# SiLU kept in its PSUM bank, GpSimd making the rests, and 23 divided down products in place of 15: an attention and mixture-of-experts kernel

## The chip, the cores and the metric

One core of a Trainium2 chip runs the whole program. The metric is the device time of one execution in microseconds. The engines are TensorE (PE in the profile; its weight loads are PEld), VectorE (DVE), ScalarE (ACT), GpSimd (POOL) and SyncE (SP), which issues most transfers. They run their own streams in order and wait for each other by semaphores.

## The reference

Inputs are x of 8 batches x 256 tokens x 128 features and a context of 8 x 256 x 96. All is float32. What is computed, cut to what matters:

```
x = x + attention(layernorm(x), ctx)       # scores normalised by their mean and variance over a batch, then softmax
h = layernorm(x)
out = x + swiglu(h @ sw1 + sb1) @ sw2 + sb2                       # the shared expert
        + sum over 8 experts e: cw[e] * (swiglu(h @ rw1[e] + rb1[e]) @ rw2[e] + rb2[e])
swiglu(a, b) = silu(a) * b;  cw: softmax of the router's logits, kept for the best two experts, else 0
```

All eight experts are computed for all tokens and weighted with cw, most of which is 0.

## The kernel before

The 2048 tokens go in four chunks c of 512 (two batches). For each chunk the nine experts e (e = 0 is the shared one) follow one another, which gives 36 slots n = 9c + e. The attention, second normalisation and router of the next chunks are laid between the slots, by the tables PE_AT, ACT_AT, DVE_AT and POOL_AT: a piece, the slot at which it stands and a place in it. Each engine's order is thus fixed in the source, and what an engine issues waits for what is queued ahead of it.

One slot n does this:

- TensorE: hidden(n, 0) and hidden(n, 1), the two halves of the hidden layer, of 128 x 512 into a PSUM bank each. To keep precision at the faster format fp32r, a factor is split into a head (rounded to fp32r) and a rest (what the rounding left), and three products are summed: head x head, rest x head, head x rest.
- ScalarE: expert_silu, the SiLU of the first half, into an SBUF buffer silu (L588).
- VectorE: expert_gate. First the weighting, silu times cw_all (L873), then the gate, (second half + bias) x silu, into act (L881). For e = 0 there is no weighting. For e = 1 in chunks 1 to 3, first_expert_gate makes the gate first (L858) and the weighting after it (L862).
- TensorE, three slots later (two near the end): down(n), which adds act times w2 to the bank OUT_B. A direct down is one float32 product (two rows in the trace). A divided one is three fp32r products and needs act_head, cast by ScalarE (L580), and act_rest, subtracted by VectorE (L890), besides w2_head and w2_rest (L886).

DIVIDED lists the divided downs: 8, 9, 10, 11, 16, 17, 18, 25, 26 and 27 to 32. The other 21 are direct. Down 33 stands in slot 35 between hidden(35, 0) and hidden(35, 1); the downs of slots 34 and 35 go straight to token order at the end (L998, w_sb<-act with 128 x 128).

Around this stand the steps that the prediction names: x_copy and the other copies of the next chunk's inputs, scores_average (the mean of the scores, bank<-sim_mom), scores_moments (sim_sq, sim_ex, sim_mom: small operations on VectorE, L743 to L750), normalise (xn, L541, which needs ln_shift, L722, and ln_rstd of GpSimd, L419), transpose_x2, x2_heads (ScalarE, L547) and x2_rests (VectorE, L799), router (bank<-gate_parts), router_logits to router_weights on VectorE, which ends in cw_cols (L850), and transpose_cw (L1113), whose result is written to memory and read back as cw_all, spread over all partitions. GpSimd makes powers (row_powers L410, ln_rstd L419, sim_r L425) and the rests of w1 (L434); in most slots it has nothing to do.

transpose_cw(c) stands at the end of slot 9c - 1, so chunk 1's in slot 8, chunk 2's in slot 17, chunk 3's in slot 26. The semaphores that matter: a_ps and b_ps count hidden halves, silu_sb SiLUs, scaled_sb weightings, act_sb gates, act_head_sb and act_rest_sb the parts of act, y_ps downs.

## Time and profile before

| | |
|---|---|
| median of 3 runs | 135.35 us (135.25 to 135.39) |
| the profiled execution | 135.15 us, of it span 133.4 us |
| TensorE's granted clock | 1.00 of full speed |
| busy: PE, DVE, ACT, POOL | 127.5, 107.6, 84.8, 23.9 us |
| SiLU (L588), 35 of 128 x 512 | 0.69 us each |
| weighting (L873), 26 of 128 x 512 | 0.69 us each |
| gate (L881), 32 of 128 x 512 | 0.75 us each |
| act_head (L580), act_rest (L890), 15 each | 0.62 and 0.68 us each |

A line of a timeline is one instruction or a run of equal ones: start, duration, engine, source line, operation, what it writes and reads, and in brackets the idle time of the engine before it with what ended it. TensorE's matmuls overlap in the record: one lasts 0.40 us but the next starts 0.23 us later, so starts are what to compare.

### The profile page before, as it was taken

The page shows a single profiled execution, that of the slowest core. Times are in us where ns is not written, and L with a number is a line of the kernel's source. Part 1 is how long each engine was busy: PE and PEld are TensorE (multiplying, and loading weights), DVE is VectorE, ACT ScalarE, POOL GpSimd, SP SyncE. Part 2 cuts the span into 40 slices and gives each one's busy share as a digit, 9 for nine tenths or more (in the row PEclk, how much of TensorE's full clock was granted, in tenths as well). Part 3 has the DMA queues.
Part 4 walks back from the last instruction along what each step waited for, and adds up shares of the span by engine and source line. Part 5 has one row for each costly group of instructions (what it writes and reads, how often), then busy time and mean ns, then how long its engine had stood idle before and what let it go on. Part 6 is the DMA issues. An engine that isn't in the chain of part 4 may idle for free.

```text
span 133.4 us, 2135 instructions
## 1 busy us (share of the span) xinstructions
PE 127.5 (96%) x632; PEld 96.7 (72%) x632; DVE 107.6 (81%) x313; ACT 84.8 (64%) x165; POOL 23.9 (18%) x41
## 2 busy tenths in 40 slices
PE   7899999889999999999999999999999999999992
PEld 7677796858577776686788676598677667788871
DVE  1497788696997989999759997699697879989872
ACT  1557978996265389947653299956633987647250
POOL 7184154057700020602100020001200000000000
PEclk9999999999999999999999999999999999999999
DMA  3999400002910000098000002087000207910022
GB/s 107 304 331 269 149 7 0 0 2 86 337 59 0 0 0 2 10 296 328 0 5 0 0 0 79 18 292 332 2 0 0 79 5 182 403 44 5 0 79 79
DMA packets 8828, 12.97 MB, mean 97 GB/s; under 512 B 1321, under 2 KB 6994, under 8 KB 8306
## 3 DMA queue, kind: packets, MB, share of 16 engines
q1 hardware_dynamic: 8242, 12.62, 28.1%
q10 hardware_dynamic: 576, 0.23, 0.6%
q8 instruction: 5, 0.08, 0.3%
q14 instruction: 5, 0.04, 0.1%
HBM read 11.73 MB, written 1.11 MB: 96 GB/s over the span
## 4 chain that ended last, share of the span: by engine, by line
PE 61%; issue 15%; DVE 9%; ACT 7%; POOL 6%; DVEq 0%; POOLq 0%; ACTq 0%
PE bank L998 55%; ACT prob L508 3%; POOL w_rest L434 3%; POOL ln_rstd L419 2%; PE bank L1062 1%; PE bank L1014 1%; ACT L553 1%; PE bank L1113 1%; PE bank L1090 1%; DVE x L902 1%; ACT act_head L580 1%; PE bank L1181 1%; DVE g_beats L824 1%; DVE g_rank L827 1%; ACT silu L588 1%
## 5 line engine op out<-in xcount | busy, mean ns | idle before, releaser
L588 ACT ACTIVATE silu<-bank,b_cols 128x512 f32<-128x512 f32 (+1 forms) x37 | 24.8, 676 | 23.7 <-PE bank L998 23.2
L998 PE MATMUL bank<-x_head,w_head 128*128 128x512 f32 x72 | 33.7, 468 | 0.3 <-issue 0.3
L998 PE MATMUL bank<-x_head,w_rest 128*128 128x512 f32 x72 | 28.5, 395 | 0.0
L998 PE MATMUL bank<-x_rest,w_head 128*128 128x512 f32 x72 | 28.5, 395 | 0.0
L881 DVE SCALAR_TENSOR_TENSOR act<-bank,b_cols,silu 128x512 f32<-128x512 f32 (+1 forms) x34 | 24.9, 734 | 1.3 <-DVE silu L873 0.3
L873 DVE TENSOR_TENSOR silu<-silu,cw_all 128x512 f32<-128x512 f32 (+1 forms) x28 | 18.6, 668 | 3.3 <-ACT silu L588 2.6
L998 PE MATMUL bank<-act,w_sb 128*128 128x512 f32 x38 | 19.4, 592 | 0.0
L998 PEld LDWEIGHTS bank<-x_head,w_head 128*128 128x128 f32 x72 | 13.6, 189 | 5.3 <-issue 2.7
L998 PEld LDWEIGHTS bank<-x_rest,w_head 128*128 128x128 f32 x72 | 13.6, 189 | 3.9 <-issue 1.9
L998 PEld LDWEIGHTS bank<-x_head,w_rest 128*128 128x128 f32 x72 | 13.5, 188 | 3.3
L890 DVE TENSOR_TENSOR act_rest<-act,act_head 128x512 fp32r<-128x512 f32 x15 | 10.0, 685 | 4.1 <-ACT silu L588 2.0
L580 ACT CAST act_head<-act 128x512 fp32r<-128x512 f32 x15 | 9.0, 623 | 1.2 <-DVE act L862 0.6
L419 POOL TENSOR_TENSOR ln_rstd<-ln_veps,minus_half 128x4 f32<-128x4 f32 (+1 forms) x5 | 5.2, 1037 | 23.6 <-DVE ln_veps L714 23.6
L508 ACT ACTIVATE prob<-bank,neg_max,row_scale 128x256 f32<-128x256 f32 x16 | 8.8, 565 | 0.0
L410 POOL TENSOR_TENSOR row_powers<-ln_veps,powers 128x8 f32<-128x8 f32 x4 | 6.9, 1736 | 9.3 <-DVE ln_veps L714 9.2
L998 PEld LDWEIGHTS bank<-v_sb,prob_t 128*128 128x128 f32 x64 | 7.7, 191 | 1.1 <-issue 0.9
L998 PE MATMUL bank<-v_sb,prob_t 128*128 128x128 f32 x64 | 8.1, 278 | 0.0
L998 PEld LDWEIGHTS bank<-act,w_sb 128*128 128x128 f32 x38 | 7.0, 189 | 1.5
L998 PE MATMUL bank<-u_sb,x_t 128*128 128x256 f32 x32 | 7.7, 384 | 0.2
L425 POOL TENSOR_TENSOR sim_r<-sim_veps,minus_half 128x2 f32<-128x2 f32 x4 | 2.8, 698 | 25.6 <-DVE sim_veps L763 25.6
L434 POOL TENSOR_TENSOR w_rest<-w_sb,w_head 128x768 fp32r<-128x768 f32 (+2 forms) x4 | 5.7, 1417 | 9.2 <-DVE cw_cols L850 5.8
L998 PEld LDWEIGHTS bank<-u_sb,x_t 128*128 128x128 f32 x32 | 5.9, 189 | 1.7 <-issue 0.8
(130 smaller groups left out, 219.4 us busy)
## 6 DMA issues: line engine op xcount, KB each, us to landing
cw_all<-cw_dram SPq DMA_DIRECT2D x4, 1024.0 KB, 7.0
cw_all<-cw_dram SPq DMA_DIRECT2D x4, 512.0 KB, 5.0
cw_all<-cw_dram SPq DMA_DIRECT2D x6, 256.0 KB, 3.7
x_sb<-in_x_dram SPq DMA_DIRECT2D x4, 256.0 KB, 4.2
w_sb<-in_L_ffn_rw_dram SPq DMA_DIRECT2D x1, 1024.0 KB, 7.4
ctx_sb<-in_ctx_dram SPq DMA_DIRECT2D x4, 192.0 KB, 4.2
out_dram<-x SPq DMA_DIRECT2D x3, 256.0 KB, 2.1
w_sb<-in_L_ffn_rw_dram SPq DMA_DIRECT2D x1, 512.0 KB, 7.1
```

The lines of the kernel that those rows point to most:

```text
L410: pool.tensor_tensor(row_powers[:, c % 2], ln_veps[:, 2 * (c % 2), :].unsqueeze(1).broadcast_to([P, 2, TC]), powers[:, :, :], ALU.pow).the ...
L419: pool.tensor_tensor(ln_rstd[:, t], ln_veps[:, 1, t], minus_half[:, t], ALU.pow).then_inc(ln_r[1], 1)
L425: pool.tensor_tensor(sim_r[:, :], sim_veps[:, :], minus_half[:, 0:CB], ALU.pow).then_inc(simr_sb, 1)
L434: pool.tensor_tensor(rest, whole, head.bitcast(F32), ALU.subtract).then_inc(w1_rest_sb[g], 1)
L508: return scalar.activation(prob[:, j, i, :], early(c)[j][:, i * S:(i + 1) * S], ACT.Exp, bias=neg_max[:, IB * j + i:IB * j + i + 1], scale ...
L553: scalar.activation(g_exp[:, :, :], g_z[:, :, :], ACT.Exp).then_inc(gexp_sb, 1)
L580: copy(act_head[:, n % 3, :], act[:, n % 4, :]).then_inc(act_head_sb, 1)
L588: scalar.activation(silu[:, k, cols], hid(n, 0)[:, cols], ACT.Silu, bias=b1_cols[:, 0, e:e + 1]).then_inc(silu_sb, 1)
L873: dve.tensor_tensor(silu[:, k, cols], silu[:, k, cols], cw_all[:, e - 1, cols], ALU.mult).then_inc(scaled_sb, 1)
L881: dve.scalar_tensor_tensor(act[:, n % 4, cols], hid(n, 1)[:, cols], b1_cols[:, 1, e:e + 1], silu[:, k, cols], ALU.add, ALU.mult).then_inc( ...
L890: dve.tensor_tensor(act_rest[:, n % 3, :], act[:, n % 4, :], act_head[:, n % 3, :].bitcast(F32), ALU.subtract).then_inc(act_rest_sb, 1)
L998: return pe.matmul(dst, lhs, rhs, start=start, stop=stop, skip_group_check=True)
```

## The change

Five things are changed together.

1. The SiLU of a slot stays in the PSUM bank of its hidden half (in_bank), for n of 4 and more except the last slot, and except e = 0 and e = 1 of chunks 1 to 3. VectorE's weighting reads the bank and writes the silu buffer. The next product into that bank waits for the weighting (scaled_sb) where it waited for the SiLU. In first_expert_gate the raw gate is made in the bank of the second half.
2. 23 downs are divided: 4, 8, 9 to 13, 16, 17, 18 to 22, 25, 26 and 27 to 33. New are 4, 12, 13, 19, 20, 21, 22 and 33.
3. GpSimd makes act_rest for fourteen of them (BY_POOL: 4, 8 to 13, 17 to 22, 26), each in two halves of 256 columns. VectorE makes it for nine (16, 25, 27 to 33).
4. GpSimd makes w2_rest, in two pieces, in slot 3; VectorE made it in slot 9. ScalarE casts w2_head in slot 2, before in slots 5 and 6.
5. act_head(m) of chunks 0 to 2 stands in slot m + 2 ahead of that slot's SiLU. Before, it stood behind the SiLU of slot m + 2 or m + 1 for most m. scores_rstd moves one slot later on GpSimd.

The diff, cut to its core:

```diff
         DOWN_BEHIND, CLOSE_FROM = 3, NX * (C - 1) + 1
-        DIVIDED = [n for n in range(NX - 1, LAST - STRAIGHT)
-                   if n >= NX * (C - 1) or n % NX in ((0, 1, 2, 7, 8) if n < NX * 2 else (0, 7, 8))]
+        DIVIDED_OF = [(4, 8), (0, 1, 2, 3, 4, 7, 8), (0, 1, 2, 3, 4, 7, 8), range(NX - STRAIGHT)]
+        DIVIDED = [n for n in range(NX * C) if n % NX in DIVIDED_OF[n // NX]]
+        BY_POOL = [n for n in DIVIDED if n < NX * (C - 1) and n % NX != NX - 2]
+        BY_DVE = [n for n in DIVIDED if n not in BY_POOL]
 
         def parts_slot(m):
 
-            return m + 1 if m >= CLOSE_FROM or m % NX in (0, 2) else m + 2
+            return m + 2 if m < NX * (C - 1) else m + 1
+
+        def heads_in(n, ahead):
+
+            return [m for m in DIVIDED if parts_slot(m) == n and ahead == (m < NX * (C - 1))]
...
+        def weighted(n):
+
+            c, e = n // NX, n % NX
+            return E * c + e - c
+
+        def in_bank(n):
+
+            return FOUR_BANKS_FROM <= n < LAST and n % NX >= (1 if n < NX else 2)
...
+            def w2_rests():
+                for g, (lo, hi) in enumerate(W2_GROUPS):
+                    pool.wait_ge(w2_head_sb, g + 1)
+                    pool.tensor_tensor(w2_rest[:, lo:hi, :], w2_sb[:, lo:hi, :], w2_head[:, lo:hi, :].bitcast(F32), ALU.subtract).then_inc(w2_rest_sb, 1)
+
+            def act_rests(m):
+                pool.wait_ge(act_head_sb, divided(m))
+                for cols in (slice(0, N // 2), slice(N // 2, N)):
+                    pool.tensor_tensor(act_rest[:, m % 3, cols], act[:, m % 4, cols], act_head[:, m % 3, cols].bitcast(F32), ALU.subtract).then_inc(pool_rest_sb, 1)
...
+                if n == 3:
+                    w2_rests()
+                for m in pool_rests_in(n):
+                    act_rests(m)
...
                 for _, cols in parts(n):
-                    scalar.activation(silu[:, k, cols], hid(n, 0)[:, cols], ACT.Silu, bias=b1_cols[:, 0, e:e + 1]).then_inc(silu_sb, 1)
+                    silu_out = hid(n, 0)[:, cols] if in_bank(n) else silu[:, k, cols]
+                    scalar.activation(silu_out, hid(n, 0)[:, cols], ACT.Silu, bias=b1_cols[:, 0, e:e + 1]).then_inc(silu_sb, 1)
...
-                        dve.tensor_tensor(silu[:, k, cols], silu[:, k, cols], cw_all[:, e - 1, cols], ALU.mult).then_inc(scaled_sb, 1)
+                        dve.tensor_tensor(silu[:, k, cols], hid(n, 0)[:, cols] if in_bank(n) else silu[:, k, cols], cw_all[:, e - 1, cols], ALU.mult).then_inc(scaled_sb, 1)
...
                     if n == FOUR_BANKS_FROM:
                         pe.wait_ge(scaled_sb, BY_PRODUCT)
-                    pe.wait_ge(silu_sb, n - 1)
+                    if in_bank(n - 2):
+                        pe.wait_ge(scaled_sb, weighted(n - 2))
+                    else:
+                        pe.wait_ge(silu_sb, n - 1)
```

ScalarE between the output bias of chunk 1 and the x2_head of chunk 3 (slots 21 to 23), before:

```order
L596 ACTIVATE out_t<-bank4,sb2_col 128x512 [waits tok_ps,y_ps]
L588 ACTIVATE silu<-bank0,b1_cols 128x512 [waits act_sb,a_ps]
L541 ACTIVATE xn<-x1,ln_shift,ln_rstd 128x128 [waits x2t_ps,shift_sb]
L541 ACTIVATE xn<-x1,ln_shift,ln_rstd 128x128 x3
L588 ACTIVATE silu<-bank3,b1_cols 128x512 [waits act_sb,a_ps]
L547 CAST x2_head<-bank7 128x512 [waits x2t_ps]
```

and after (the line numbers are those of the changed source):

```order
L622 ACTIVATE out_t<-bank4,sb2_col 128x512 [waits tok_ps,y_ps]
L605 CAST act_head<-act 128x512 [waits y_ps,act_sb]
L614 ACTIVATE bank0<-bank0,b1_cols 128x512 [waits act_sb,a_ps]
L566 ACTIVATE xn<-x1,ln_shift,ln_rstd 128x128 [waits x2t_ps,shift_sb]
L566 ACTIVATE xn<-x1,ln_shift,ln_rstd 128x128 x3
L605 CAST act_head<-act 128x512 [waits y_ps,act_sb]
L614 ACTIVATE bank3<-bank3,b1_cols 128x512 [waits act_sb,a_ps]
L572 CAST x2_head<-bank7 128x512 [waits x2t_ps]
```

Two casts, act_head of 19 and of 20, now stand ahead of the SiLUs of slots 21 and 22.

VectorE in slots 34 and 35, before; the first row is the gate of slot 33, the second the final addition of chunk 2:

```order
L881 SCALAR_TENSOR_TENSOR act<-bank1,b1_cols,silu 128x512 [waits y_ps,b_ps,scaled_sb]
L897 TENSOR_TENSOR x1<-bank7,x1 128x512 [waits tok_ps]
L873 TENSOR_TENSOR silu<-silu,cw_all 128x512 [waits cw_in3,silu_sb]
L881 SCALAR_TENSOR_TENSOR act<-bank2,b1_cols,silu 128x512 [waits y_ps,b_ps,scaled_sb]
L873 TENSOR_TENSOR silu<-silu,cw_all 128x256 [waits cw_in3,silu_sb] x2
```

and after:

```order
L906 SCALAR_TENSOR_TENSOR act<-bank1,b1_cols,silu 128x512 [waits y_ps,b_ps,scaled_sb]
L918 TENSOR_TENSOR x1<-bank7,x1 128x512 [waits tok_ps]
L898 TENSOR_TENSOR silu<-bank3,cw_all 128x512 [waits cw_in3,silu_sb]
L911 TENSOR_TENSOR act_rest<-act,act_head 128x512 [waits act_head_sb]
L906 SCALAR_TENSOR_TENSOR act<-bank2,b1_cols,silu 128x512 [waits y_ps,b_ps,scaled_sb]
L898 TENSOR_TENSOR silu<-silu,cw_all 128x256 [waits cw_in3,silu_sb] x2
```

The rest of act 33 is new between the weighting and the gate of slot 34; TensorE's down 33 waits for it.

GpSimd in slots 2 to 10, before:

```order
L434 TENSOR_TENSOR w1_rest<-w1_sb,w1_head 128x768 [waits w1_head_sb3]
L419 TENSOR_TENSOR ln_rstd<-ln_veps,minus_half 128x4 [waits xn_ready,ln2_var]
L425 TENSOR_TENSOR sim_r<-sim_veps,minus_half 128x2 [waits prob_sb,simvar_sb]
L410 TENSOR_TENSOR row_powers<-ln_veps,powers 128x8 [waits negmax_sb,ln1_var]
L419 TENSOR_TENSOR ln_rstd<-ln_veps,minus_half 128x4 [waits xn_ready,ln2_var]
```

and after:

```order
L430 TENSOR_TENSOR ln_rstd<-ln_veps,minus_half 128x4 [waits xn_ready,ln2_var]
L450 TENSOR_TENSOR w2_rest<-w2_sb,w2_head 128x640 [waits w2_head_sb]
L450 TENSOR_TENSOR w2_rest<-w2_sb,w2_head 128x512 [waits w2_head_sb]
L455 TENSOR_TENSOR act_rest<-act,act_head 128x256 [waits act_head_sb]
L455 TENSOR_TENSOR act_rest<-act,act_head 128x256
L436 TENSOR_TENSOR sim_r<-sim_veps,minus_half 128x2 [waits prob_sb,simvar_sb]
```

Both pieces of w2_rest and the rest of act 4 stand between ln_rstd of chunk 1 and sim_r of chunk 2.

## Rows read from the trace of the kernel before

**Rows 1.** the page's busy times: us, share of the span, instructions

```profile
PE 127.5 (96%) x632; PEld 96.7 (72%) x632; DVE 107.6 (81%) x313; ACT 84.8 (64%) x165; POOL 23.9 (18%) x41
```

**Rows 2.** timeline of TensorE: start us, us, engine, line, operation; a direct down

```profile
47.55 1.02 PE L998 MATMUL bank<-act,w_sb 128*128 128x512 f32 x2
...
48.64 0.40 PE L998 MATMUL bank<-x_rest,w_head 128*128 128x512 f32 x1
```

**Rows 3.** timeline of TensorE, slot 11: a divided down

```profile
59.99 0.39 PE L998 MATMUL bank<-act_head,w_head 128*128 128x512 f32 x1
...
60.92 0.39 PE L998 MATMUL bank<-x_rest,w_head 128*128 128x512 f32 x1
```

**Rows 4.** timeline, end of slot 8: VectorE, then TensorE

```profile
50.63 0.23 DVE L850 TENSOR_TENSOR cw_cols<-cw_cols 128x64 f32<-128x64 f32 x1
...
50.92 0.65 PE L1113 MATMUL bank<-ident,cw_cols 128*112 128x128 f32 x4
```

**Rows 5.** timeline, slots 13 to 15: VectorE, then TensorE

```profile
71.30 0.68 DVE L799 TENSOR_TENSOR x_rest<-bank,x_head 128x512 fp32r<-128x512 f32 x1
...
75.45 0.19 DVE L810 TENSOR_TENSOR logits<-bank,logits_part 128x32 f32<-128x32 f32 x1
...
74.78 1.02 PE L998 MATMUL bank<-act,w_sb 128*128 128x512 f32 x2
75.79 0.37 PE L998 MATMUL bank<-sim_mom,mean_of_partitions 128*128 128x16 f32 x2
```

**Rows 6.** timeline, slots 18 and 19: VectorE, then TensorE

```profile
85.85 0.69 DVE L890 TENSOR_TENSOR act_rest<-act,act_head 128x512 fp32r<-128x512 f32 x1 [0.94 <-ACT silu L588]
...
86.69 0.48 PE L998 MATMUL bank<-act_head,w_head 128*128 128x512 f32 x1 [0.23 <-DVE act_rest L890]
...
87.47 1.95 PE L998 MATMUL bank<-v_sb,prob_t 128*128 128x128 f32 x16
```

**Rows 7.** timeline, slots 21 to 26: ScalarE, VectorE, TensorE

```profile
94.43 1.65 ACT L541 ACTIVATE xn<-x,ln_shift,ln_rstd 128x128 f32<-128x128 f32 x4 [1.48 <-DVE ln_shift L722]
...
98.08 0.68 DVE L799 TENSOR_TENSOR x_rest<-bank,x_head 128x512 fp32r<-128x512 f32 x1
...
98.91 0.25 PE L998 MATMUL bank<-gate_parts,x_head 128*128 128x16 f32 x1
...
106.22 1.02 PE L998 MATMUL bank<-act,w_sb 128*128 128x512 f32 x2
107.08 0.60 PE L1113 MATMUL bank<-ident,cw_cols 128*112 128x128 f32 x4
```

**Rows 8.** groups by line and shape: count, busy us, mean ns of one, idle before

```profile
L580 ACT CAST act_head<-act 128x512 fp32r<-128x512 f32 x15 | 9.0, 623 | 1.2 <-DVE act L862 0.6 <-DVE act L881 0.5
...
L434 POOL TENSOR_TENSOR w_rest<-w_sb,w_head 128x256 fp32r<-128x256 f32 x1 | 0.7, 729 | 0.0
```

**Rows 9.** timeline, slots 34 and 35: VectorE, then TensorE

```profile
126.08 0.68 DVE L873 TENSOR_TENSOR silu<-silu,cw_all 128x512 f32<-128x512 f32 x1
...
126.68 1.02 PE L998 MATMUL bank<-act,w_sb 128*128 128x512 f32 x2
```

**Rows 10.** timeline of places where GpSimd and VectorE meet

```profile
7.25 3.26 POOL L410 TENSOR_TENSOR row_powers<-ln_veps,powers 128x8 f32<-128x8 f32 x2 [3.50 <-DVE ln_veps L714]
...
9.91 0.17 DVE L743 TENSOR_TENSOR sim_sq<-sim_stats 128x8 f32<-128x8 f32 x1
...
35.16 1.01 POOL L419 TENSOR_TENSOR ln_rstd<-ln_veps,minus_half 128x4 f32<-128x4 f32 x1 [0.28 <-DVE ln_veps L714]
...
36.46 0.69 DVE L873 TENSOR_TENSOR silu<-silu,cw_all 128x512 f32<-128x512 f32 x1
...
41.34 0.69 DVE L799 TENSOR_TENSOR x_rest<-bank,x_head 128x512 fp32r<-128x512 f32 x1 [0.76 <-ACT x_head L547]
...
53.56 0.69 DVE L873 TENSOR_TENSOR silu<-silu,cw_all 128x512 f32<-128x512 f32 x1
...
53.73 2.02 POOL L410 TENSOR_TENSOR row_powers<-ln_veps,powers 128x8 f32<-128x8 f32 x1 [5.73 <-DVE ln_veps L714]
```

More of the change, by code:

```diff
@@ L307, in xattn_moe_kernel, with pool_rests_in, dve_rests_in @@
         DOWN_BEHIND, CLOSE_FROM = 3, NX * (C - 1) + 1
-        DIVIDED = [n for n in range(NX - 1, LAST - STRAIGHT)
-                   if n >= NX * (C - 1) or n % NX in ((0, 1, 2, 7, 8) if n < NX * 2 else (0, 7, 8))]
+        DIVIDED_OF = [(4, 8), (0, 1, 2, 3, 4, 7, 8), (0, 1, 2, 3, 4, 7, 8), range(NX - STRAIGHT)]
+        DIVIDED = [n for n in range(NX * C) if n % NX in DIVIDED_OF[n // NX]]
+        BY_POOL = [n for n in DIVIDED if n < NX * (C - 1) and n % NX != NX - 2]
+        BY_DVE = [n for n in DIVIDED if n not in BY_POOL]
         def parts_slot(m):
-            return m + 1 if m >= CLOSE_FROM or m % NX in (0, 2) else m + 2
-        def parts_place(m):
-            if m >= CLOSE_FROM:
-                return "between"
-            return {7: "first", 2: "last"}.get(m % NX, "between")
-        def divided_in(n, places):
-            return [m for m in range(n - 2, n) if m in DIVIDED and parts_slot(m) == n and parts_place(m) in places]
+            return m + 2 if m < NX * (C - 1) else m + 1
+        def heads_in(n, ahead):
+            return [m for m in DIVIDED if parts_slot(m) == n and ahead == (m < NX * (C - 1))]
+        def pool_rests_in(n):
+            return [m for m in BY_POOL if parts_slot(m) == n]
+        def dve_rests_in(n):
+            return [m for m in BY_DVE if parts_slot(m) == n]
+        def weighted(n):
[3 more added lines that the diff above has]
+            return FOUR_BANKS_FROM <= n < LAST and n % NX >= (1 if n < NX else 2)
         def downs_in(n):
@@ L662, in _ @@
                     pieces[piece](k)
-                for m in divided_in(n, ("first",)):
+                for m in heads_in(n, True):
                     act_heads(m)
@@ L666, in _ @@
                     expert_silu(c, e)
-                for m in divided_in(n, ("between",)):
+                for m in heads_in(n, False):
                     act_heads(m)
@@ L674, in _ @@
                     pieces[piece](k)
-                for m in divided_in(n, ("last",)):
-                    act_heads(m)
-                if n in (5, 6):
-                    w2_heads(n - 5)
+                if n == 2:
+                    w2_heads(0)
+                    w2_heads(1)
             out_bias(C - 1)
@@ L876, in expert_gate @@
                     if e >= 1:
-                        dve.wait_ge(scaled_sb, E * c + e + h - c)
+                        dve.wait_ge(scaled_sb, weighted(n) + h)
                     dve.wait_ge(b_ps, n + 1)
@@ L882, in expert_gate @@
                                              ALU.add, ALU.mult).then_inc(act_sb, 1)
-            def w2_rests():
-                dve.wait_ge(w2_head_sb, len(W2_GROUPS))
-                dve.tensor_tensor(w2_rest[:, :, :], w2_sb[:, :, :], w2_head[:, :, :].bitcast(F32), ALU.subtract).then_inc(w2_rest_sb, 1)
             def act_rests(n):
@@ L977, in between @@
                 def between():
-                    for m in divided_in(n, ("first", "between")):
+                    for m in dve_rests_in(n):
                         act_rests(m)
@@ L985, in _ @@
                     expert_gate(c, e, between)
-                for m in divided_in(n, ("last",)):
-                    act_rests(m)
                 if n == 0:
                     first_statistics(2)
-                if n == NX:
-                    w2_rests()
                 run(n, 2)
@@ L1159, in down @@
                 if n in DIVIDED:
-                    pe.wait_ge(w2_rest_sb, 1)
-                    pe.wait_ge(act_rest_sb, divided(n))
+                    pe.wait_ge(w2_rest_sb, len(W2_GROUPS))
+                    if n in BY_POOL:
+                        pe.wait_ge(pool_rest_sb, 2 * (BY_POOL.index(n) + 1))
+                    else:
+                        pe.wait_ge(act_rest_sb, BY_DVE.index(n) + 1)
                     mm(OUT_B[:, :], w2_head[:, e, :], act_head[:, k, :], first, False)
```

10 lines of the change are left out of this document (5 added, 5 removed).

## The prediction

> **What bounds the kernel now.** I read the page first: TensorE is marked busy for 96% of the span, VectorE for 81%, ScalarE for 64%, GpSimd for 18% [rows 1]. A TensorE mark covers pipelined ends, so the price of its work has to be taken from start to start in the timeline. I then followed TensorE's timeline through the four chunks and looked, at each place where it starts late, for the row that ended just before on another engine. Between those places TensorE simply issues one product after another, and there a cheaper product is worth its whole difference. At those places a chain on VectorE or ScalarE decides, and what TensorE saves ahead of it becomes waiting.
>
> Number the 36 expert slots n = 0 to 35 (nine per chunk; down(n) is the second product of slot n).
>
> **The gain that the change is after.** A direct down and the first of three hidden products behind it take 48.64 - 47.55 = 1.09 us [rows 2]. The same with a divided down takes 60.92 - 59.99 = 0.93 us [rows 3]. A division gives 0.16 us. Eight more are divided: downs 4, 12, 13, 19, 20, 21, 22 and 33, at most 8 x 0.16 = 1.28 us. Which of these reach the end?
>
> *Down 4* stands in slot 7. The combine-weight transposes of chunk 1 start at 50.92, 0.06 us after VectorE finishes cw_cols (50.63 + 0.23) [rows 4]: they wait for it. VectorE's order from chunk 1's x2_rest to that cw_cols is the same in both kernels and holds no act_rest. This saving becomes waiting: 0.
>
> *Downs 12 and 13.* Down 12 starts at 74.78 and would be through at 75.64 (1.09 less one hidden product, a quarter of the 0.93, = 0.86), but scores_average starts only at 75.79, 0.15 us after the second logits addition ends at 75.64 [rows 5]. It waits for logits, which follow x2_rest (71.30) on VectorE through work that is the same in both kernels. Down 13 lies between there and the next cw_cols, a chain of the same kind. Savings: 0 and 0. VectorE can begin x2_rest slightly earlier with no rests ahead of it; I leave out that 0.1 us.
>
> *Down 16* is no new division, and it keeps its wait: its act_rest stays on VectorE, ends at 86.54, and TensorE goes on at 86.69 [rows 6]. So 0.15 us is what passes from a VectorE end to a TensorE start.
>
> *Downs 19 and 20* stand ahead of chunk 3's router, which starts at 98.91, again 0.15 us after x2_rest ends (98.08 + 0.68) [rows 7]. There the two engines are level, so earlier arrival of TensorE gives nothing, unless x2_rest comes earlier. Ahead of x2_rest lie, on ScalarE, the normalisation at 94.43 and the SiLU of slot 22, now with an act_head between them (0.62 us, [rows 8]). The normalisation itself waited 1.48 us for VectorE's ln_shift [rows 7], and VectorE no longer makes the rests of 17 and 18 ahead of it, but waits longer for SiLU 19 behind act_head 17. The bounds are 0.4 us earlier and 0.6 us later; I take 0, since the two edits are of one size.
>
> *Downs 21 and 22* come behind that router. The next join, the transposes of chunk 3's weights, starts at 107.08, exactly when the direct down from 106.22 is through (+ 0.86) [rows 7]: TensorE is not waiting there. Both savings count: -0.31 us.
>
> *Down 33* is in the tail and costs. Slot 35 has it between its two hidden products. Direct, it starts at 126.68 and needs only act 33, long made. Divided, it needs act_rest(33), which VectorE makes in slot 34 behind the final addition and behind the weighting that starts at 126.08 [rows 9]. Weighting 0.68 and rest 0.68 bring 127.4, plus 0.15 to TensorE: 127.53. TensorE idles 0.85 us. A divided down after an idle takes 87.47 - 86.69 = 0.78 us [rows 6], against 0.86 direct. Everything behind it (the second hidden half, the last gate, the output bias, the token transposes) hangs on it: **+0.77 us**. VectorE's own tail moves by 0.68 us at least, so there is no way around it.
>
> **What moves at no price on the path.** The rests of fourteen downs go from VectorE to GpSimd in halves of 256 columns, 0.73 us each [rows 8], so 1.46 us a slot of some 2.3 us. The heads now stand ahead of the SiLU of slot n+2; in most slots ScalarE waits for TensorE there, and this hides them. If GpSimd were late, down 19 would feel it first, since its rest is queued behind ln_rstd of chunk 3; I find it ready about 0.3 us early. SiLU written in its bank makes hidden(n, 0) wait for the weighting of n-2 instead of its SiLU. The closest case is slot 10, whose product comes about 0.3 us after weighting 8 ends (53.56 + 0.69 = 54.25 [rows 10]): hidden. No row shows ScalarE writing to PSUM; between its row with an SBUF target (0.62 us, [rows 8]) and the 0.69 us of a SiLU I allow 0.07 us either way for each, mostly off the path, and take 0. The Trainium skill (PSUM — Partial Sum Buffer, § Specifications (TRN2)) calls ScalarE faster to PSUM than to SBUF; no row here shows it, and no term uses it.
>
> **The price of sharing.** GpSimd and VectorE disturb each other. A row_powers takes 1.63 us elsewhere and 2.02 us when it starts at 53.73 inside the weighting of 53.56 to 54.25, which has two SBUF inputs [rows 10]: the second comer pays 0.38 us. The change takes one SBUF input from most weightings, so GpSimd is mostly safe. But does VectorE pay when GpSimd came first? One row says no: GpSimd runs two row_powers from 7.25 to 10.51 (3.26 us, 1.63 each), and VectorE's sim_sq at 9.91, with two SBUF inputs, takes its usual 0.17 us [rows 10]. Yet those read eight columns, not 256 to 640. The new w2_rests (640 columns, at most 2.5 x 0.73 = 1.8 us) run straight behind ln_rstd of chunk 1, from 35.16 + 1.01 = 36.2, while VectorE wants ln_shift and the two-input weighting at 36.46 [rows 10]. The bounds are 0 and about 4 us (rival one). I take one collision at the only measured price, +0.38 us.
>
> **Sum.** -0.31 + 0.77 + 0 + 0.38 = +0.84 us. The profiled execution had 135.15 us, 133.4 of it span; it would become 134.2 of span and 136.0 in all. The median of the three runs is 0.20 us above it, and what is asked is set against that median: 135.35 + 0.84 = **136.2 us**.
>
> **Rival one: the port holds VectorE back (slower by more).** GpSimd's w2_rest starts at about 36.2 and holds ln_shift and weighting 3 until it ends, near 37.8: 1.3 us. VectorE had 0.76 us of idle ahead of x2_rest at 41.34 [rows 10], so 0.6 us arrives on the chain that ends in [rows 4]; if the second half of w2_rest slips in first, 1.8 us. Then the four small statistics operations, each with two SBUF inputs, meet the act_rests of 4 and 12, each a possible wait of one half, 0.73 us: 0.3 to 2 us more. Together +1.2 to +4 us over the +0.46 without sharing: 137.0 to 139.8, middle 138.2 us. The speaking row is GpSimd's own delay, which shows that something exclusive is held; against it speaks sim_sq at 9.91. The Trainium skill (SBUF — State Buffer, § Who interferes with whom) has this very rule: a VectorE instruction with two SBUF inputs and a GpSimd instruction that reads SBUF contend, and the second to start blocks fully. By that rule this rival comes true; the trace agrees for GpSimd as second comer (0.38 us) and has no long GpSimd read first.
>
> **Rival two: the savings get through (faster).** If the chains of [rows 4], [rows 5] and [rows 7] follow TensorE when it comes earlier, all seven savings ahead of the tail count: 7 x 0.16 = 1.1 us, less 0.77 us, and no sharing: 135.0 us. It decides at the cw_cols of chunks 1 and 2: only if VectorE ends them 0.2 to 0.3 us earlier. VectorE does the same operations there, which speaks against it; only faster reads of a bank, or earlier starts after chunk 2's rests are gone, speak for it.
>
> **Rival three: nothing measurable.** No sharing at all and x2_rest of chunk 3 up to 0.4 us earlier: between 135.2 and 135.6 us.
>
> **How the numbers follow.** A measurement of this kernel tells about 0.2%, 0.27 us, from no change. Forecast (135.6 to 136.8 us): 0.36. Rival one: 0.36. Rival two: 0.12, of which 0.02 within 0.27 us. Rival three: 0.14, of which 0.12 within and 0.02 faster. The rest, 0.02, is slower. Faster 0.12, within 0.14, slower 0.74. The range reaches from 135.0, rival two's time, to 138.9, which leaves out the upper fifth of rival one and half of rival two.
>
> **What would show it.** In the changed profile TensorE idles about 0.85 us before the down product between the two hidden halves of slot 35; that row decides the tail term. The waits before chunk 1's and 2's cw_cols transposes grow by what was saved. An act_rest on GpSimd takes 0.73 us a half. Rival one shows as VectorE rows near 36.4 starting over 1 us late or lasting over 1 us, and x2_rest of chunk 1 after 41.9. I am wrong if chunk 1's transposes come at 50.9 or earlier with no idle, or if the tail's down finds its rest ready.

## The result, and the profile after

| | before | after |
|---|---|---|
| median | 135.37 us (135.25 to 135.43, 4 runs) | 138.14 us (137.96 to 138.44, 4 runs) |
| ratio | | 1.0209, 95% interval 1.0190 to 1.0228 |
| profiled execution | 135.15 us, span 133.4 us | 137.96 us, span 136.1 us |

The changed kernel is 2.77 us slower, where the prediction had 0.84. The page's busy times of the changed kernel:

```profile
PE 127.1 (93%) x640; PEld 98.5 (72%) x640; DVE 106.8 (78%) x306; ACT 88.3 (65%) x173; POOL 45.8 (34%) x71
```

Beside [rows 1], VectorE has slightly less to do, GpSimd almost twice as much, and TensorE's share falls to 93%: the time that was added is waiting, not work.

**Where the time goes.** The opening, behind the first loads, takes a slightly different time in each execution: the score average of chunk 1 (TensorE's second product on sim_mom) starts between 18.22 and 19.16 us in the profiled ones. So I count every place from that start, which lies ahead of all changes. It is at 18.49 us before and at 18.66 us after.

| from the score average of chunk 1 to ... | before | after | difference |
|---|---|---|---|
| weight transposes of chunk 1 | 32.43 | 33.43 | +1.00 |
| weight transposes of chunk 2 | 62.78 | 64.90 | +2.12 |
| router of chunk 3 | 80.42 | 82.71 | +2.29 |
| weight transposes of chunk 3 | 88.59 | 90.56 | +1.97 |
| last addition on VectorE | 111.73 | 114.36 | +2.63 |

So the difference has four parts, each read from one execution of each kernel: 2.12 us in chunks 1 and 2, 0.17 us ahead of chunk 3's router, -0.32 us behind it, and 0.66 us in the tail.

**Chunk 1, first place.** Timeline of GpSimd and VectorE in the changed kernel, slot 3. A line is start, duration, engine, source line, operation; x2 means two instructions in one row.

```profile
35.33 1.01 POOL L430 TENSOR_TENSOR ln_rstd<-ln_veps,minus_half 128x4 f32<-128x4 f32 x1 [0.27 <-DVE ln_veps L739]
36.31 3.32 POOL L450 TENSOR_TENSOR w_rest<-w_sb,w_head 128x640 fp32r<-128x640 f32 x2
...
35.88 0.75 DVE L906 SCALAR_TENSOR_TENSOR act<-bank,b_cols,silu 128x512 f32<-128x512 f32 x1
36.55 1.32 DVE L747 SCALAR_TENSOR_TENSOR ln_shift<-ln_mv,ln_rstd 128x4 f32<-128x4 f32 x1
37.79 0.68 DVE L898 TENSOR_TENSOR silu<-silu,cw_all 128x512 f32<-128x512 f32 x1
38.51 0.75 DVE L906 SCALAR_TENSOR_TENSOR act<-bank,b_cols,silu 128x512 f32<-128x512 f32 x1
```

ln_shift writes four columns. It took 0.15 us and takes 1.32 us. It ends at 37.87. GpSimd's first w2_rest (640 columns) started at 36.31 and takes 1.55 us, to 37.86. The weighting that started at 36.46 [rows 10] starts at 37.79. And the second w2_rest, which began while that weighting ran, is slow itself: 1.82 us for 512 columns, where the larger one took 1.55. The gate at 38.51 starts inside that second w2_rest, but one of its inputs is in a bank, and it takes its usual 0.75 us. By shape, over the span:

```profile
L450 POOL TENSOR_TENSOR w_rest<-w_sb,w_head 128x512 fp32r<-128x512 f32 x1 | 1.8, 1815 | 0.0
...
L450 POOL TENSOR_TENSOR w_rest<-w_sb,w_head 128x640 fp32r<-128x640 f32 x1 | 1.5, 1546 | 0.0
```

**Chunks 1 and 2, second place.** The score moments are four operations on VectorE of eight columns. Timeline of the changed kernel: first act_rest(4) on GpSimd with chunk 2's moments on VectorE, then act_rest(12) and (13) with chunk 3's, and last the score average of TensorE that stands at 75.79 in [rows 5].

```profile
42.86 1.41 POOL L455 TENSOR_TENSOR act_rest<-act,act_head 128x256 fp32r<-128x256 f32 x2 [3.23 <-ACT act_head L605]
...
43.20 0.40 DVE L768 TENSOR_TENSOR sim_sq<-sim_stats 128x8 f32<-128x8 f32 x1
43.64 0.65 DVE L770 SCALAR_TENSOR_TENSOR sim_ex<-sim_stats,sim_sq 128x8 f32<-128x8 f32 x1
44.21 0.15 DVE L772 TENSOR_TENSOR sim_mom<-sim_stats,row_powers 128x8 f32<-128x8 f32 x1
44.40 0.17 DVE L775 TENSOR_TENSOR sim_mom<-sim_ex,row_powers 128x8 f32<-128x8 f32 x1
...
72.81 2.81 POOL L455 TENSOR_TENSOR act_rest<-act,act_head 128x256 fp32r<-128x256 f32 x4 [2.23 <-ACT act_head L605]
...
73.64 0.61 DVE L768 TENSOR_TENSOR sim_sq<-sim_stats 128x8 f32<-128x8 f32 x1
74.28 0.66 DVE L770 SCALAR_TENSOR_TENSOR sim_ex<-sim_stats,sim_sq 128x8 f32<-128x8 f32 x1
74.86 0.15 DVE L772 TENSOR_TENSOR sim_mom<-sim_stats,row_powers 128x8 f32<-128x8 f32 x1
75.05 0.59 DVE L775 TENSOR_TENSOR sim_mom<-sim_ex,row_powers 128x8 f32<-128x8 f32 x1
...
78.09 0.37 PE L1015 MATMUL bank<-sim_mom,mean_of_partitions 128*128 128x16 f32 x2 [1.41 <-DVE logits L835]
```

Before the change each of them takes 0.16 or 0.17 us. Here sim_sq ends at 43.60, when GpSimd's first half is through (42.86 and half of 1.41), and sim_ex at 44.29, when the second is (44.27). Then the next two have their usual 0.15 and 0.17 us. Beside four halves, three of the four operations are held. The score average behind them, at 75.79 in [rows 5], is at 78.09.

The two places can be told apart by x2_rest, which lies between them. That of chunk 1 (41.82 for 41.34 before) is 0.31 us late, counted, and the transposes behind the moments are 1.00 us late. That of chunk 2 (72.24 for 71.30) is 0.77 us late, and the transposes behind the next moments 2.12.

**The tail** looks as forecast. TensorE around down 33, then VectorE:

```profile
128.50 0.39 PE L1015 MATMUL bank<-x_head,w_rest 128*128 128x512 f32 x1
129.56 0.47 PE L1015 MATMUL bank<-act_head,w_head 128*128 128x512 f32 x1 [0.67 <-DVE act_rest L911]
...
128.14 0.68 DVE L898 TENSOR_TENSOR silu<-bank,cw_all 128x512 f32<-128x512 f32 x1
128.74 0.68 DVE L911 TENSOR_TENSOR act_rest<-act,act_head 128x512 fp32r<-128x512 f32 x1
```

The direct down of [rows 9] had no wait; the divided one waits for act_rest(33). It starts 1.06 us behind the product ahead of it, where products otherwise start 0.23 us apart: 0.83 us late, and the forecast had 0.85.

### The profile page after: what moved, and what is told of

Same layout as the page of the kernel before. It is cut to its first block, busy times and chain, and to the rows that moved or that the text cites. A ratio compares the mean times of both kernels' runs of the same rounds, so it can differ in the third digit from the quotient of the medians.

```text
span 136.1 us, 2198 instructions
## 1 busy us (share of the span) xinstructions
PE 127.1 (93%) x640; PEld 98.5 (72%) x640; DVE 106.8 (78%) x306; ACT 88.3 (65%) x173; POOL 45.8 (34%) x71
## 4 chain that ended last, share of the span: by engine, by line
PE 48%; DVE 19%; issue 14%; ACT 10%; POOL 6%; DVEq 0%; ACTq 0%; POOLq 0%
PE bank L1015 43%; ACT prob L533 3%; POOL w_rest L450 2%; DVE x L810 2%; DVE silu L898 2%; POOL ln_rstd L430 2%; DVE ln_stats L727 2%; PE bank L1130 1%; ACT act_head L605 1%; PE bank L1079 1%; PE bank L1031 1%; DVE x_rest L824 1%; POOL act_rest L455 1%; ACT L578 1%; ACT xn L566 1%
## 5 line engine op out<-in xcount | busy, mean ns | idle before, releaser
L455 POOL TENSOR_TENSOR act_rest<-act,act_head 128x256 fp32r<-128x256 f32 x28 | 19.8, 732 | 31.4 <-ACT act_head L605 31.2
L614 ACT ACTIVATE bank<-bank,b_cols 128x512 f32<-128x512 f32 x25 | 16.5, 659 | 20.6 <-PE bank L1015 20.4
L898 DVE TENSOR_TENSOR silu<-bank,cw_all 128x512 f32<-128x512 f32 x25 | 17.1, 685 | 4.0 <-ACT bank L614 2.7
L605 ACT CAST act_head<-act 128x512 fp32r<-128x512 f32 x23 | 14.2, 619 | 1.5 <-DVE act L906 1.2
L1015 PE MATMUL bank<-act,w_sb 128*128 128x512 f32 x22 | 11.2, 592 | 0.0
L1015 PE MATMUL bank<-act_head,w_head 128*128 128x512 f32 x23 | 9.6, 419 | 1.0 <-DVE act_rest L911 0.9
L1015 PE MATMUL bank<-act_head,w_rest 128*128 128x512 f32 x23 | 9.1, 396 | 0.0
L1015 PE MATMUL bank<-act_rest,w_head 128*128 128x512 f32 x23 | 9.1, 395 | 0.0
L614 ACT ACTIVATE silu<-bank,b_cols 128x512 f32<-128x512 f32 (+1 forms) x12 | 7.6, 653 | 2.1 <-PE bank L1015 2.1
L757 DVE BATCH_NORM_STATS2 sim_stats<-bank 128x6 f32<-128x256 f32 x16 | 6.0, 419 | 3.4 <-PE bank L1015 3.3
```

The costliest lines, as they stand in the source:

```text
L455: pool.tensor_tensor(act_rest[:, m % 3, cols], act[:, m % 4, cols], act_head[:, m % 3, cols].bitcast(F32), ALU.subtract).then_inc(pool_res ...
L605: copy(act_head[:, n % 3, :], act[:, n % 4, :]).then_inc(act_head_sb, 1)
L614: scalar.activation(silu_out, hid(n, 0)[:, cols], ACT.Silu, bias=b1_cols[:, 0, e:e + 1]).then_inc(silu_sb, 1)
L757: own(dve.bn_stats(sim_stats[:, IB * j + i].rearrange("p h k -> p (h k)"), scores[:, i * S:(i + 1) * S]))
L898: dve.tensor_tensor(silu[:, k, cols], hid(n, 0)[:, cols] if in_bank(n) else silu[:, k, cols], cw_all[:, e - 1, cols], ALU.mult).then_inc(s ...
L1015: return pe.matmul(dst, lhs, rhs, start=start, stop=stop, skip_group_check=True)
```

## The experiments

Two theories. **Port:** VectorE operations with two inputs in SBUF stand still while GpSimd runs an instruction that reads SBUF, which costs about 2.1 us in chunks 1 and 2. **The rest of the change:** act_heads ahead of the SiLUs, the new wait for weightings, or savings lost. Beside the measured times stands the last VectorE addition counted as in the table above, against 111.73 us before, since the opening moves it from run to run: "counted +0.75" is 112.48 us. A counted time comes from a single execution, so it has no interval, and a difference of a tenth or two says little. The kernel before ran beside each of them, with medians of 135.32 to 135.35 us.

### GpSimd reads in slot 3, alone

```
+ if n == 3:   # GpSimd's stream of the kernel before; unread is a buffer of its own
+     unread[:, 0:5, :] = w1_sb[:, 0:5, 0:D] - w1_sb[:, 0:5, D:2 * D]    # 640 columns
+     unread[:, 0:4, :] = w1_sb[:, 0:4, 0:D] - w1_sb[:, 0:4, D:2 * D]    # 512 columns
```

> The kernel before, with two more GpSimd subtractions (640 and 512 columns, both inputs in SBUF) in slot 3, right behind ln_rstd of chunk 1. Nothing reads their result and no other engine gets a wait. Port theory: they take about 3.3 us from 36.2 on, ln_shift lasts over 1 us in place of 0.15, weighting 3 starts 1.2 us late, and the 0.76 us of idle ahead of x2_rest absorbs part: slower by 0.5 to 1.1 us. Rival theory (the loss of chunk 1 comes from ScalarE's w2_heads in slot 2, or from the new wait of hidden products for weightings): no engine but GpSimd has more to do, so within 0.2 us of the kernel before and ln_shift at 0.15 us.

Measured: 136.08 us, ratio 1.0049 (1.0030 to 1.0068); counted +0.75. GpSimd and VectorE in slot 3, and VectorE in slot 10:

```profile
36.13 1.55 POOL L476 TENSOR_TENSOR unread<-w_sb 128x640 f32<-128x640 f32 x1
...
36.37 1.33 DVE L726 SCALAR_TENSOR_TENSOR ln_shift<-ln_mv,ln_rstd 128x4 f32<-128x4 f32 x1
...
61.41 0.69 DVE L866 TENSOR_TENSOR act<-act,cw_all 128x512 f32<-128x512 f32 x1 [1.98 <-DMA cw_all<-cw_dram]
```

ln_shift is at 1.33 us with nothing else changed. Work whose result nobody reads slows the kernel, so the collision alone is a cause. At the weight transposes of chunk 1 it is only 0.34 us: the 0.76 us of idle ahead of x2_rest [rows 10] takes most of the rest. It is 0.71 us at those of chunk 2, and there another cause stands between: VectorE waited 1.98 us for the transfer of chunk 1's weights into cw_all (61.41), for which it didn't wait before. Its issues start 0.27 us later than before (55.69 for 55.42), but the two pieces of 256 KB landed 5.8 us after issue in place of 3.6. Why isn't settled; the direct price is 0.34 us.

### w2_rest in nine pieces

```
- pool.tensor_tensor(w2_rest[:, lo:hi, :], ...)                       # 640 and 512 columns
+ for e in range(lo, hi): pool.tensor_tensor(w2_rest[:, e, :], ...)   # 128 columns each
```

> The changed kernel, with w2_rest made in nine GpSimd subtractions of 128 columns in place of two of 640 and 512. If VectorE is held back until the single GpSimd instruction ends: ln_shift lasts 0.5 us or less in place of 1.32, since one piece takes 0.35 to 0.45 us, and chunk 1's combine-weight transposes start 0.5 to 0.9 us earlier than in the changed kernel (52.09). If GpSimd keeps the port as long as it has instructions queued: ln_shift lasts 2 us or more, and the whole is slower than the changed kernel. If the port plays no part: no change, 138.1 us.

Measured: 138.09 us, ratio 1.0205 (1.0178 to 1.0231), as the changed kernel. GpSimd's nine pieces in one row, and VectorE:

```profile
36.30 4.30 POOL L451 TENSOR_TENSOR w_rest<-w_sb,w_head 128x128 fp32r<-128x128 f32 x9
42.85 1.41 POOL L456 TENSOR_TENSOR act_rest<-act,act_head 128x256 fp32r<-128x256 f32 x2 [2.25 <-ACT act_head L606]
...
36.54 0.23 DVE L748 SCALAR_TENSOR_TENSOR ln_shift<-ln_mv,ln_rstd 128x4 f32<-128x4 f32 x1
...
42.88 0.72 DVE L769 TENSOR_TENSOR sim_sq<-sim_stats 128x8 f32<-128x8 f32 x1
43.63 0.65 DVE L771 SCALAR_TENSOR_TENSOR sim_ex<-sim_stats,sim_sq 128x8 f32<-128x8 f32 x1
```

ln_shift is at 0.23 us: the hold lasts as long as the single GpSimd instruction, not as long as its queue. Half of my expectation fell, though. The transposes are still at 52.09. VectorE now reaches the moments at 42.88, 0.32 us earlier, and stands there until act_rest(4) is through at 44.27, the time at which it was through before. The second collision hides the first.

### Downs 4, 12 and 13 direct

```
- DIVIDED_OF = [(4, 8), (0, 1, 2, 3, 4, 7, 8), (0, 1, 2, 3, 4, 7, 8), range(NX - STRAIGHT)]
+ DIVIDED_OF = [(8,), (0, 1, 2, 7, 8), (0, 1, 2, 3, 4, 7, 8), range(NX - STRAIGHT)]
```

> The changed kernel with downs 4, 12 and 13 direct, so that GpSimd has no act_rest beside the score statistics of chunks 2 and 3. Port theory: the moments' small operations are back at 0.17 us each, chunk 3's sim_mom and the transposes of chunk 2's weights come about 1.1 us earlier (83.56 to about 82.4), the changed kernel loses 1.0 to 1.3 us: 136.8 to 137.1 us. Rival, that the savings of these three downs had reached the end: 0.3 to 0.5 us slower than the changed kernel. Rival, that ScalarE's heads ahead of SiLU cost there: also earlier, but with the moments' operations still at 0.4 to 0.6 us.

Measured: 136.01 us, ratio 1.0046 (1.0012 to 1.0081); counted +0.55, where the changed kernel has +2.63. VectorE's moments of chunk 3:

```profile
73.40 0.17 DVE L768 TENSOR_TENSOR sim_sq<-sim_stats 128x8 f32<-128x8 f32 x1
73.60 0.17 DVE L770 SCALAR_TENSOR_TENSOR sim_ex<-sim_stats,sim_sq 128x8 f32<-128x8 f32 x1
```

They are back at 0.17 us, and the weight transposes of chunk 2 come at +0.03 of the kernel before (+2.12 in the changed one). More came back than the 1.0 to 1.3 us that I expected, because I had split chunk 1's loss between two collisions and the one at the moments carries nearly all of it. Three divisions that could save 0.48 us at the most cost 2.1 us. This run takes the heads of 4, 12 and 13 away too, so it can't separate the port from the heads; the next two do.

### Reads, and writes, beside the moments

```
+ if n in (5, 14):   # GpSimd's stream of the kernel before, behind x2_rest of chunks 1 and 2
+     two times (n = 5) or four times (n = 14):
+         unread[:, 0:2, :] = w1_sb[:, 0:2, 0:D] - w1_sb[:, 0:2, D:2 * D]    # the first kernel
+         memset(unread[:, 0:5, :], 0)                                       # the second, in its place
```

> The kernel before, with unread GpSimd subtractions of 256 columns (both inputs in SBUF) behind x2_rest of chunk 1 (two of them) and of chunk 2 (four), so that they run beside the four small operations of the score moments. No other engine has more work or another wait. Port theory: in chunk 1 about +0.4 us (moments from 42.73, the second subtraction ends near 43.6), in chunk 2 row_max comes near 75 in place of 73.25 and sim_mom's matmul 1.2 to 1.8 us after 75.79; together 1.4 to 2.2 us slower than the kernel before: 136.8 to 137.6 us. Rival theory (the loss of these places in the changed kernel comes from act_heads 4, 12, 13 ahead of the SiLUs, or from waits of TensorE for weightings): within 0.2 us of the kernel before.

> As the run with unread subtractions at the moments, but GpSimd fills the same buffer with a constant (memset of 640 columns, about 0.7 us each by the smaller memsets: 256 columns take 0.31 us) in place of subtracting: it writes SBUF and reads nothing. If reads hold the port: moments stay at 0.17 us and the time within 0.2 us of the kernel before. If any GpSimd access to SBUF holds VectorE back: 1 us or more slower, as in the other run.

Reads: 137.48 us, ratio 1.0165 (1.0142 to 1.0189); counted +1.88. Writes: 136.12 us, ratio 1.0060 (1.0037 to 1.0083); counted +0.09. By its median the run with writes misses my 0.2 us; its moments are as expected. Chunk 3's moments, first beside reads:

```profile
72.63 3.17 POOL L478 TENSOR_TENSOR unread<-w_sb 128x256 f32<-128x256 f32 x4 [8.10 <-DVE x_rest L804]
...
73.26 0.17 DVE L748 TENSOR_TENSOR sim_sq<-sim_stats 128x8 f32<-128x8 f32 x1
73.46 0.73 DVE L750 SCALAR_TENSOR_TENSOR sim_ex<-sim_stats,sim_sq 128x8 f32<-128x8 f32 x1
74.12 0.16 DVE L752 TENSOR_TENSOR sim_mom<-sim_stats,row_powers 128x8 f32<-128x8 f32 x1
74.31 0.71 DVE L755 TENSOR_TENSOR sim_mom<-sim_ex,row_powers 128x8 f32<-128x8 f32 x1
```

and beside writes:

```profile
72.56 2.71 POOL L478 MEMSET unread<- 128x640 f32 x4 [8.08 <-DVE x_rest L804]
...
73.20 0.17 DVE L748 TENSOR_TENSOR sim_sq<-sim_stats 128x8 f32<-128x8 f32 x1
73.41 0.17 DVE L750 SCALAR_TENSOR_TENSOR sim_ex<-sim_stats,sim_sq 128x8 f32<-128x8 f32 x1
73.49 0.16 DVE L752 TENSOR_TENSOR sim_mom<-sim_stats,row_powers 128x8 f32<-128x8 f32 x1
73.69 0.17 DVE L755 TENSOR_TENSOR sim_mom<-sim_ex,row_powers 128x8 f32<-128x8 f32 x1
```

With reads alone, the kernel before loses 1.90 us by the weight transposes of chunk 2; the changed kernel lost 2.12 there. ScalarE's heads aren't needed for it. Beside 2.71 us of writes nothing is held. Operations get through where one read ends: sim_sq and the first sim_mom started within the last 0.11 us of a subtraction and took their usual time. The two others started just behind the beginning of one, and took 0.73 and 0.71 us, about as long as the subtraction (0.73 us).

One thing stays open. The run with writes took 0.77 us more than the kernel before by the medians, but only 0.09 us of it lies behind chunk 1's score average. In its profiled execution that place came 0.47 us later, and 2.28 us lay outside the span, against 1.75. The second goes with the kernel: all four executions with writes have 2.27 to 2.33 us outside the span, all four with reads 2.22 to 2.32, eight of the ten with unread work in slot 3 2.0 to 2.2, while all others, the changed kernel too, have about 1.8. So the medians of the three kernels with the buffer unread are 0.3 to 0.5 us too high for what happens inside, and the counted times are what to go by. Neither part has to do with the moments, and I don't know the cause of either.

**All kernels together.** The 14 profiled kernels have more of these meetings than the runs were built for. VectorE operations with both inputs in SBUF that start inside a GpSimd subtraction with 0.22 us or more of it left: 53, and every one ends behind the subtraction. Operations with one input in a bank, in the same position: 157, none slower by more than 0.02 us. So it takes two inputs in SBUF, as the theory says. But its other half, any instruction of GpSimd that reads SBUF, is too wide: 80 operations with both inputs in SBUF start inside a pow of GpSimd, and none is slowed. One of the changed kernel starts 0.04 us behind the beginning of a pow:

```profile
20.85 0.70 POOL L430 TENSOR_TENSOR ln_rstd<-ln_veps,minus_half 128x2 f32<-128x2 f32 x1 [1.16 <-DVE ln_veps L739]
...
20.89 0.17 DVE L786 TENSOR_TENSOR sim_avg_sq<-sim_avg 128x2 f32<-128x2 f32 x1
```

### The SiLU in its bank, alone

The edit is the part of the change with in_bank, and the raw gate in its bank, on the kernel before; DIVIDED and GpSimd's work are as they were.

> The kernel before with the SiLU result left in its bank, the weighting reading it there and the hidden products waiting for weightings; no division moved or added, no work on GpSimd. Prediction's reading: this wait is hidden, 0 to 0.1 us either way (135.2 to 135.5 us). If the wait of hidden(n,0) for weighting n-2 or for a bank costs, it is here: 0.3 us or more slower, with idle of TensorE ahead of hidden products. ScalarE's SiLU takes 0.66 us in place of 0.69.

Measured: 135.10 us, ratio 0.9990 (0.9976 to 1.0004); counted -0.20. The new waits are hidden, as the prediction had it. Whether it gains something can't be told from no change by the ratio.

### Down 33 direct

```
- ..., range(NX - STRAIGHT)]
+ ..., range(NX - STRAIGHT - 1)]
```

> The changed kernel with down 33 direct, as before the change. The prediction's tail term says 0.75 us less than the changed kernel (137.4 us), with no idle of TensorE ahead of down 33. Rival: the last weightings of VectorE bound the tail anyway, and it gains less than 0.3 us.

Measured: 137.15 us, ratio 1.0143 (1.0113 to 1.0172), 0.99 us under the changed kernel; counted +1.94 for +2.63, so 0.69 us. TensorE issues the direct down without a wait:

```profile
128.57 0.39 PE L1015 MATMUL bank<-x_head,w_rest 128*128 128x512 f32 x1
128.80 1.02 PE L1015 MATMUL bank<-act,w_sb 128*128 128x512 f32 x2
```

### Mended: 4, 12, 13 and 33 direct

Two kernels with these four downs direct, the first with w2_rest in nine pieces, the second with the two long ones.

> The changed kernel with downs 4, 12, 13 and 33 direct and w2_rest in nine pieces of 128 columns: what is left of the change is the SiLU in its bank, GpSimd's rests of the other downs, and downs 19 to 22 divided. By the parts: 136.01 (downs 4, 12, 13 direct) less 0.65 for down 33, less 0 to 0.3 us for w2's pieces, so 135.0 to 135.4 us, at the kernel before or just under it. If the three causes overlap (a mended place uncovers another wait): 135.6 us or more.

> The changed kernel with downs 4, 12, 13 and 33 direct, and w2_rest as the change has it, in two long GpSimd subtractions. Against the same with nine pieces (134.89 us) it prices the collision that the prediction took at 0.38 us: ln_shift back at 1.32 us, chunk 1's combine-weight transposes about 0.3 us later (as in the run with unread subtractions in slot 3, 51.25 against 50.92), and, if nothing behind absorbs it, 0.3 to 0.4 us slower: 135.2 us. If chunk 2's joins absorb it, as the rows of the run with 4, 12 and 13 direct suggest: 134.9 to 135.0 us.

Measured: 134.89 us, ratio 0.9969 (0.9954 to 0.9984), counted -0.36, a little better than the 135.0 to 135.4 us expected; and 135.37 us, ratio 1.0007 (0.9992 to 1.0022), counted -0.13. With the moments free, w2's pieces are worth 0.23 us counted (0.48 by the medians), where they were worth nothing in the changed kernel. And with the pieces, what is left of the change is now faster than the kernel before, by 0.3%.

### Two more divisions, and one less

Downs 23 and 24 divided as well (DIVIDED_OF[2] = range(NX)), then the same with down 20 direct.

> The run after_mended with downs 23 and 24 divided too, their rests on GpSimd. Both stand behind chunk 3's router, where TensorE waits for nothing, so by the prediction's rule for 21 and 22 both savings reach the end: 0.16 us each, 134.6 us. Rival: cw_cols of chunk 3, which ended 0.5 us ahead of its transposes, or a weighting held by GpSimd's four more subtractions takes it back: no change or slower than 134.9 us.

> As after_mended_23_24 but with down 20 direct. That takes act_head(20) from between the normalisation and SiLU 22 of ScalarE, behind which VectorE waited 1.39 us ahead of weighting 22: weighting 22 and x2_rest of chunk 3 come 0.3 to 0.5 us earlier, the router 0.2 to 0.3 us earlier, 134.3 to 134.5 us. Rival: the router then waits for the longer direct down 20 or for x2_head, and it is as after_mended_23_24 or 0.1 us slower.

Measured: 135.69 us, ratio 1.0032 (1.0016 to 1.0047), counted +0.39; and 135.14 us, ratio 0.9992 (0.9977 to 1.0007), counted -0.07. Both expectations fell: 134.6 and 134.3 to 134.5 us. I had just named the port as the cause, and still priced two divisions at TensorE alone, with GpSimd's subtractions only as the rival. GpSimd's rests of 23 and 24, VectorE's router operations, and the transposes, in the second kernel:

```profile
101.54 1.43 POOL L456 TENSOR_TENSOR act_rest<-act,act_head 128x256 fp32r<-128x256 f32 x2 [1.20 <-ACT act_head L606]
105.16 1.43 POOL L456 TENSOR_TENSOR act_rest<-act,act_head 128x256 fp32r<-128x256 f32 x2 [2.19 <-ACT act_head L606]
...
102.35 0.90 DVE L847 TENSOR_TENSOR g_diff<-logits 128x256 f32<-128x256 f32 x1
...
105.20 0.78 DVE L872 TENSOR_TENSOR cw_cols<-g_p,g_inv 128x64 fp32r<-128x64 f32 x1
105.90 0.73 DVE L874 TENSOR_TENSOR cw_cols<-g_p,g_inv 128x32 f32<-128x32 f32 x1
...
106.95 0.65 PE L1131 MATMUL bank<-ident,cw_cols 128*112 128x128 f32 x4 [0.68 <-DVE cw_cols L876]
```

g_diff takes 0.90 us for 0.41, two writes of cw_cols 0.78 and 0.73 us for 0.22 and 0.18, and TensorE waits 0.68 us. The first kernel has the same three durations. Down 20 gave more than the 0.2 to 0.3 us that I expected at the router: without its head between the normalisation and SiLU 22, the router is at -0.57 us, where the first kernel has -0.06 and the mended one +0.01. The waits for cw_cols take most of that back.

### The router's operations left alone

```
- DIVIDED_OF[2] = (0, 1, 2, 3, 4, 7, 8)    # of after_mended
+ DIVIDED_OF[2] = (0, 1, 3, 4, 7, 8)       # down 20 direct
```

> As after_mended, with down 20 direct and downs 23 and 24 direct again. In after_mended_20 the router of chunk 3 came 0.58 us earlier than in after_mended (both counted from chunk 1's score average), and this was lost by GpSimd's rests of 23 and 24, which held g_diff (0.90 us for 0.41) and two writes of cw_cols (0.78 and 0.73 us for 0.22 and 0.18). Port theory: without these two rests those operations are back at 0.41, 0.22 and 0.18 us, the transposes of chunk 3's weights come about 0.5 us earlier than in after_mended, and the time is 134.2 to 134.6 us, 0.5% under the kernel before. Rival (the router's lead is lost in any case, because the products behind it are bound by TensorE or by a copy): 134.9 us as after_mended.

Measured: 134.46 us, ratio 0.9945 (0.9924 to 0.9966); counted -0.98. The same operations of VectorE:

```profile
102.02 0.41 DVE L847 TENSOR_TENSOR g_diff<-logits 128x256 f32<-128x256 f32 x1
...
104.80 0.23 DVE L872 TENSOR_TENSOR cw_cols<-g_p,g_inv 128x64 fp32r<-128x64 f32 x1
104.95 0.19 DVE L874 TENSOR_TENSOR cw_cols<-g_p,g_inv 128x32 f32<-128x32 f32 x1
```

They are at their own durations, the transposes of chunk 3 are at -0.88 (the mended kernel has -0.26), and this kernel beats all others: 0.86 us under the kernel before, with 18 divided downs in place of 15, and GpSimd's pieces of w2_rest short. Against the mended kernel it differs in down 20 alone, which is worth 0.43 us by the medians. Leaving 23 and 24 direct takes away ScalarE's heads as well as GpSimd's rests; that the rests are what cost is read from the durations, and no run separates the two here. One collision is left in it, as in every kernel with GpSimd's rests: ln_shift of chunks 2 and 3 takes 0.50 and 0.51 us in place of 0.16, each behind a rest. No run tries it without.

## Why the prediction was wrong, by its own steps

| step | forecast | measured | by |
|---|---|---|---|
| a division saves | 0.16 us where nothing waits | -0.32 us for 21 and 22 | the changed kernel behind the router |
| downs 4, 12, 13, 19, 20 | 0 | no saving arrives | the waits behind cw_cols and x2_rest |
| x2_rest of chunk 3 | 0 (-0.4 to +0.6) | +0.17 us | from chunk 2's transposes to the router, changed kernel |
| tail, down 33 | +0.77 us | +0.66 us, 0.69 us back when undone | down 33 direct |
| SiLU in its bank | 0 | -0.20 us, within the error | that part alone |
| **sharing** | **+0.38 us (0 to 4)** | **+2.12 us** | all of chunks 1 and 2; reads alone +1.90 there, writes alone +0.10 |
| sum of the savings, x2_rest, tail and sharing | +0.84 us | +2.63 us counted, +2.77 by the medians | |

**The step that failed is the price of sharing**, and it failed in three ways. First the witness: sim_sq at 9.91, unslowed beside row_powers [rows 10]. I noted that those read eight columns, and let the row decide all the same. GpSimd's pow takes 1.63 us over eight columns, a subtraction of 640 columns 1.55 us, so the time of the pow can't be spent on reading. It was the wrong witness, as the 80 operations above show. That a pow holds the port only for a moment fits them; a subtraction of eight columns, which would tell its width from its kind, was not run. Second the price: 0.38 us was what GpSimd paid as the second to come. What a small VectorE operation pays as the second is the remainder of GpSimd's subtraction: with 1.30 us of it left, 0.15 us became 1.32. Third the count: I took one collision, although the paragraph on rival one listed the others (ln_shift, the weighting, four small operations twice).

The Trainium skill (SBUF — State Buffer, § Who interferes with whom) states that a VectorE instruction with two SBUF inputs contends with a GpSimd instruction that reads SBUF, and not with one that only writes it. The trace agrees for subtractions and memsets: 0.17 us became 0.73 beside the first, and stayed 0.17 beside the second. It doesn't agree for a pow, which reads SBUF and slowed none of 80 such operations; there the measurement decides. The same section calls the shared ports an exclusive lock; that the second to start blocks fully, for the whole instruction of the other, it states of VectorE's 2-port modes. ln_shift shows it here for a scalar_tensor_tensor too: 1.32 us with the long piece, 0.23 us with the short ones.

**Rival one came true, with its price.** It had 137.0 to 139.8 us with a middle of 138.2; the result is 138.14. Its parts were less good than its sum. They add to 0.9 to 3.8 us as written, not 1.2 to 4, and 138.2 is the middle of the former range. It expected 0.6 us or more from w2_rest, which is worth 0.23 to 0.34 us, and 0.3 to 2 us from the moments, which cost nearly 2. One of its signs missed: x2_rest of chunk 1 starts at 41.82, not after 41.9, since the moments that cost most lie behind it. It had the same chance as the forecast, 0.36, so the range held the result, but the number given was the other one.

**Downs 4, 12 and 13** were read correctly as absorbed savings. What I failed to ask was what an absorbed saving may cost: it brings a head, a rest and a reader of SBUF to the very chain that absorbs it. All 2.1 us are lost on that chain, which ends in cw_cols and logits and runs on VectorE.

**Down 20** was a bound whose middle I took as zero. The "0.6 later" was the nearer end for that one: dividing it costs 0.5 to 0.6 us at the router, as two pairs of kernels that differ in down 20 alone show (-0.06 and -0.57, +0.01 and -0.58). In the mended kernel its act_head, 0.60 us, stands between the normalisation and SiLU 22; with down 20 direct the SiLU follows at once. In the changed kernel the transposes of x2 come 0.32 us earlier than before, counted from the weight transposes of chunk 2 (98.11 - 83.56 against 96.14 - 81.27), and that hides part of it; +0.17 is left. Sharing is in that figure too: ln_shift of chunk 3 is held 0.35 us behind a rest, while GpSimd's ln_rstd ahead of it got 0.38 us shorter.

**Rival two** had a true part. In the mended kernel the transposes of chunk 2 come 0.24 us early, and so does x2_rest ahead of them; that was the condition it named. Fewer rests on VectorE are the likely reason, but no run shows it alone.

**The tail** was right, with a slip: 126.08 + 0.68 + 0.68 + 0.15 is 127.59, not 127.53, which would make the term 0.83 and the whole 0.90 us.

## What to carry to other kernels

Work moved to an idle GpSimd isn't free for VectorE: list VectorE's operations with two SBUF inputs that run beside it, the smallest ones first, and charge each with the rest of one GpSimd instruction (here subtractions of 128 to 640 columns; the pows, 0.7 to 1.6 us long, held nothing). Where these operations stand on a chain that another engine waits for, make the GpSimd instructions short, or put them elsewhere, or have no such work there. And a saving on TensorE that would only become waiting should not be bought at all: its helpers load the chain that TensorE waits for.
